# Rotary attention stage of a two-layer decoder: the clip-and-causal pass and the exponential take an earlier place in the frame

## The chip, the cores and the metric

The kernel runs on one core of a Trainium2 chip. The metric is the device time of one execution in microseconds (us), lower being better. Three timed runs of the kernel before gave 3401.52, 3405.44 and 3408.87 us; the median is 3405.44 us.

## The reference, cut to what matters

The kernel computes a decoder of two layers for 32 sequences of 112 tokens with 256 features. Each layer has a self attention, a cross attention to a context of 375 rows, and a mixture of experts. The change touches only the self attention of the second layer, which the kernel calls `RotaryAttention`. Its reference is:

```python
def _L1_attn_ref(x, W_DQ, W_UQ, W_QR, W_DKV, W_UK, W_UV, W_KR, W_O):
    # x: the layer-normalised stream, 32 x 112 x 256; 16 heads of 16 features, 8 of them rotary ones beside
    c_q = x @ W_DQ                      # 64 wide
    Qc, Qr = heads(c_q @ W_UQ), rope(heads(c_q @ W_QR))
    c_kv = x @ W_DKV                    # 64 wide
    Kc, V = heads(c_kv @ W_UK), heads(c_kv @ W_UV)
    Kr = rope((x @ W_KR)[:, None])      # one for all heads
    scores = einsum('bhqd,bhkd->bhqk', concat(Qc, Qr), concat(Kc, Kr))
    scores = clip(scores, -80.0, 80.0)
    scores = where(causal, scores, -inf)
    weights = softmax(scores / sqrt(24), axis=-1)
    attn = einsum('bhqk,bhkd->bhqd', weights, V)
    return merge(attn) @ W_O            # added to x by the caller
```

## The kernel before, in words

The stages of the decoder follow one another, with a barrier of all engines between them. `RotaryAttention` is one such stage, from about 1567 to 1877 us of the profiled span. It is streamed: sequence b passes through 17 named pieces, and a frame is one pass through the list of pieces, each for a sequence of its own. A piece of age a works in frame e on sequence b = e - a. There are 32 sequences and ages up to 4, so there are 36 frames. Four are written out in front, 28 run in a loop and four follow to drain; a piece whose sequence does not exist in a frame is left out.

The order is written out by hand in the list `Flow` (line 1464). There is no planner. Every engine walks through the same list and does its own share of each piece, so the list sets the order inside each engine's queue, and semaphores join the engines. For the change these shares matter:

- TensorE, in the order of the list: `scores` (age 2, 32 small matmuls, L1503), `q` (L1521), `turnk` (L1528, the rotary turn of the key part), `onT` (L1540), `heads` (age 3, probabilities times values, L1229), `kc` (L1521), `xT` (the transpose of the normalised input, L859), `turnq` (L1528), `v` (L1531), `c` and `kr` (L1513), `project` (L1282), `back` (L1265).
- VectorE: `stats` (L761 to L763, layer-norm statistics), `turnk` (L1595 to L1598), `scale` (L772, the normalised input that `xT` transposes), `bound` (L1583, the clip and the causal mask of all scores of a sequence in one instruction), `kc` (L1602, which adds the turned key part and frees the bank), `turnq` (L1588 to L1592), `project` (L1306), `back` (L1299, L1301).
- ScalarE: copies out of the banks, all at L885 (`q`, `onT`, `heads`, `xT`, `v`, `c`, `kr`), and `exp` (L1563, the exponential of all clipped scores of a sequence).
- GpSimd computes only the reciprocal root of the variance (L767), and SyncE has nothing to do in this stage.

Matmul results go to a ring of four banks of PSUM. The pieces `stats`, `scale`, `scores`, `bound` and `exp` take no bank of the ring. The other twelve take the banks in turn in the order of the list: `q`, `kc` and `c` the first, `turnk`, `xT` and `kr` the second, `onT`, `turnq` and `project` the third, `heads`, `v` and `back` the fourth. A piece on TensorE waits until the piece before it in its bank has been read out (`claim`, line 218). So `c` waits for VectorE's `kc`, and `v` waits for ScalarE's copy of `heads`. Where a sequence does not exist, TensorE still claims the bank and passes it on (`skip`, line 225). The scores have four banks of their own; `scores` of one sequence waits for `bound` of the sequence before it.

Of the kernel before, what the change touches and what calls it, by code (L numbers as in the profile page):

```python
# [138 lines left out]
class Chain:  # L139
# [3 lines left out]
    def __init__(self, eng, sem, once=None):  # L143
        self.eng, self.sem, self.once = eng, sem, once
        self.base = self.n = self.k = 0
# [580 lines left out]
class Phase:  # L726
# [3 lines left out]
    scale = 1.0  # L730
# [157 lines left out]
class LatentAttention(Phase):  # L888
# [4 lines left out]
    scale = XD ** -0.5 * XD ** -0.5  # L893
# [415 lines left out]
class CausalAttention(Streamed):  # L1309

    tag = "a0"
    scale = HD ** -0.5
# [142 lines left out]
class RotaryAttention(Streamed):  # L1455
# [4 lines left out]
    scale = 24 ** -0.5  # L1460

    def __init__(self, nc, G, W):
        super().__init__(nc, G, W)
        self.plan = Flow(4, [("stats", 0), ("scores", 2), ("q", 1), ("turnk", 1), ("onT", 4), ("scale", 0), ("heads", 3),
                             ("bound", 2), ("kc", 1), ("xT", 0), ("turnq", 1), ("v", 1), ("c", 0), ("kr", 0), ("exp", 2),
                             ("project", 4), ("back", 3)])

    def allocate(self, sb, sem):
# [141 lines left out]
class ContextAttention(Streamed):  # L1610

    tag = "x1"
    scale = HD ** -0.5
# [503 lines left out]
class RelativeAttention(Streamed):  # L2117
# [3 lines left out]
    scale = HD ** -0.5  # L2121
# [1014 lines left out]
```

How the kernel before makes its waits and increments, by code:

```python
    def link(self, ins):  # L168
        self.eng.wait_ge(self.sem, self.inc(ins))
# [1 line left out]
    def link_apart(self, ins):  # L171
        ins.then_inc(self.once, 1)
        self.eng.wait_ge(self.once, 1)
        self.eng.sem_clear(self.once)
# [24 lines left out]
def at_least(eng, sem, n):  # L201
    if not isinstance(n, int) or n > 0:
        eng.wait_ge(sem, n)
# [26 lines left out]
    def take(self, eng, c, e):  # L231
        eng.wait_ge(self.full[c % self.size], self.count(c, e) + 1)
        return self.banks[c % self.size]
# [4 lines left out]
    def emptied(self, eng, c, e):  # L238
        eng.wait_ge(self.free[c % self.size], self.count(c, e) + 1)
# [96 lines left out]
        @block.sync  # L336
        def _(sp):
            sp.dma_start(low["q"][0][:], t["q_aT"].rearrange("(g i) r d -> (i r) g d", i=2)).then_inc(loaded["q"], 16)
            sp.wait_ge(low_zeroed, 1)
            for i in range(2):
                sp.dma_start(low["q"][1][64 * i:64 * (i + 1), :, HD * i:HD * (i + 1)],
                             t["L0_attn_q_b"].rearrange("(g i) r d -> i r g d", i=2)[i]).then_inc(loaded["q"], 16)
            q = NB // 4
            for i in range(4):
                sp.dma_start(G["X"][0:T, i * q:(i + 1) * q, :],
                             t["x"].rearrange("b t d -> t b d")[:, i * q:(i + 1) * q, :]).then_inc(small, 16)
            sp.wait_ge(small, 64)
# [1 line left out]
        @block.scalar  # L349
        def _(act):
            act.dma_start(low["k"][0][:], t["k_aT"].rearrange("(g i) r d -> (i r) g d", i=2)).then_inc(loaded["k"], 16)
            act.wait_ge(low_zeroed, 2)
            for i in range(2):
```

## Time and profile before

| | us |
|---|---|
| median of three timed runs | 3405.44 |
| lowest and highest of them | 3401.52, 3408.87 |
| profiled execution, first to last instruction (span) | 3418.2 |
| first instruction of VectorE in the stage | 1567.07 |
| last instruction of VectorE in the stage | 1876.22 |
| one frame in the steady part | 9.0 to 9.1 |

The profiled execution is one run of its own. The profile gives its time from the first to the last instruction, 3418.2 us, and no separate time for what lies around this span. The timed runs were not profiled. A frame is the distance from the first matmul of `scores` to the first of the next frame.

### The profile page before, as it was taken

The numbers are of one execution on the slowest core, as the hardware profiler recorded it, in microseconds if no ns is written. First come the engines' busy times: TensorE is split into PE (matmuls) and PEld (weight loads), VectorE is DVE, ScalarE is ACT, GpSimd is POOL, SyncE is SP. The second block draws the span as 40 slices with busy tenths as digits, with TensorE's granted clock in tenths as the row PEclk, the third lists the DMA queues.
The fourth block names the chain that finished last, engine by engine and source line by source line (L and its number), as shares of the span: only waits on it lengthen the run. The fifth ranks groups of instructions, "written<-read, shape, count | busy, mean of one in ns | idle before, by whom it ended". The sixth has DMA issues, their size and how long they took to land. (4 is left out here: it accounts for less than half of the span.)

```text
span 3418.2 us, 78608 instructions
## 1 busy us (share of the span) xinstructions
PE 3017.6 (88%) x28488; PEld 2122.1 (62%) x28488; DVE 2357.3 (69%) x4873; ACT 1668.7 (49%) x3240; POOL 836.4 (24%) x1093
## 2 busy tenths in 40 slices
PE   6997999999999987998998799999997999955771
PEld 6886555555555555666776466666665877744661
DVE  5997566666666654676786566666663989965666
ACT  3775555555555551333444244444443877742440
POOL 0000344444444440000000100000000144445551
PEclk9998999999999997999999799999997999977996
DMA  8000555545555530000000333323322777755557
GB/s 194 0 0 2 146 145 145 144 142 144 144 145 145 145 92 1 1 0 1 0 0 2 71 68 68 70 63 68 69 55 70 218 224 227 223 169 169 156 158 233
DMA packets 316466, 351.64 MB, mean 103 GB/s; under 512 B 104552, under 2 KB 290032, under 8 KB 316112
## 3 DMA queue, kind: packets, MB, share of 16 engines
q1 hardware_dynamic: 175456, 173.66, 19.4%
q10 hardware_dynamic: 127776, 141.34, 14.9%
q0 software_dynamic: 13008, 33.56, 2.9%
q8 instruction: 151, 2.47, 0.3%
q14 instruction: 75, 0.61, 0.1%
HBM read 109.49 MB, written 207.08 MB: 93 GB/s over the span
## 5 line engine op out<-in xcount | busy, mean ns | idle before, releaser
L1090 ACT ACTIVATE x_probs<-x_held,x_minus_top 112x488 f32<-112x488 f32 x256 | 177.5, 694 | 281.8 <-DVE x_minus_top L1144 281.8
L1863 DVE TENSOR_REDUCE x_top<-x_scores 112x2 f32<-112x750 f32 x256 | 231.1, 935 | 118.7 <-PE x_scores L1720 114.3
L767 POOL TENSOR_TENSOR x_rstd<-x_var,g_minus_half 112x1 f32<-112x1 f32 x128 | 74.3, 580 | 743.6 <-DVE x_var L763 743.6
L966 POOL TENSOR_TENSOR x_probs<-x_probs,x_inverse 112x488 f32<-112x488 f32 x256 | 250.9, 1002 | 10.0
L1005 PE MATMUL x_ring<-w_xkv,x_kv 128*122 128x512 f32 x512 | 242.4, 596 | 1.2 <-PEq L229 1.2
L998 PE MATMUL x_ring<-x_kv,w_xkv 128*128 128x488 f32 x512 | 233.7, 589 | 1.8 <-ACT x_kv L1065 1.1
L1138 DVE SCALAR_TENSOR_TENSOR x_held<-x_scores,x_keep 112x976 f32<-112x976 f32 x128 | 150.4, 1175 | 108.1 <-PE x_scores L1018 100.0
L1829 ACT ACTIVATE x_probsT<-x_scores 125x1792 f32<-125x1792 f32 x96 | 159.9, 1665 | 79.4 <-PE x_scores L1739 79.4
L961 POOL TENSOR_TENSOR x_inverse<-x_sums,x_minus_one 112x2 f32<-112x2 f32 x128 | 94.8, 740 | 419.3 <-ACT x_probs L1090 419.3
L1720 PE MATMUL x_scores<-x_slots 32*112 32x375 f32 x1024 | 171.5, 538 | 27.1 <-DVE x_top L1863 14.0
L767 POOL TENSOR_TENSOR a_rstd<-a_var,g_minus_half 112x1 f32<-112x1 f32 x64 | 35.3, 551 | 586.4 <-DVE a_var L763 586.4
L2873 POOL DMA_INDIRECT expert_replies<-m_rows,m_reply_of x143 | 139.8, 978 | 111.7 <-ACT m_rows L2965 74.9
L998 PEld LDWEIGHTS x_ring<-x_kv,w_xkv 128*128 128x128 f32 x512 | 92.8, 191 | 117.4 <-issue 111.6
L885 ACT ACTIVATE x_v<-x_ring 122x512 f32<-122x512 f32 (+1 forms) x224 | 112.6, 503 | 107.7 <-PE x_ring L1005 85.6
L2751 DVE SCALAR_TENSOR_TENSOR g_residual<-m_out,m_gate,g_residual 112x256 f32 (+1 forms) x256 | 108.0, 478 | 66.2 <-PE m_out L2587 64.6
L1143 DVE TENSOR_REDUCE x_top<-x_held 112x2 f32<-112x976 f32 x128 | 149.8, 1170 | 4.4
L1005 PEld LDWEIGHTS x_ring<-w_xkv,x_kv 128*122 128x122 f32 x512 | 89.6, 185 | 93.4 <-issue 92.9
L885 ACT ACTIVATE x_probsT<-x_ring 122x448 f32<-122x448 f32 x256 | 124.9, 545 | 44.9 <-PE x_ring L1026 44.8
L1026 PEld LDWEIGHTS x_ring<-g_constants,x_probs 112*122 112x122 f32 x1024 | 109.7, 140 | 46.2 <-issue 35.4
L1018 PE MATMUL x_scores<-x_k,x_q 64*112 64x488 f32 x512 | 130.4, 607 | 1.0 <-PEq L229 1.0
L1043 PEld LDWEIGHTS x_ring<-x_probsT,x_v 122*64 122x64 f32 x2048 | 101.3, 139 | 47.3 <-issue 47.3
L1026 PE MATMUL x_ring<-g_constants,x_probs 112*122 112x112 f32 x1024 | 121.4, 262 | 6.9 <-POOL x_probs L966 4.3
(417 smaller groups left out, 7545.4 us busy)
## 6 DMA issues: line engine op xcount, KB each, us to landing
expert_slots<-d_empty ACTq DMA_DIRECT2D x32, 3612.0 KB, 14.4
by_position<-r_by_position SPq DMA_DIRECT2D x64, 784.0 KB
r_bias<-by_position SPq DMA_DIRECT2D x64, 392.0 KB
m_rows<-expert_slots SPq DMA_DIRECT2D x143, 129.0 KB
x_kq_swapped<-x_kq_raw ACTq DMA_DIRECT2D x64, 243.5 KB
x_slots<-x_kq SPq DMA_DIRECT2D x512, 30.4 KB
m_rows<-expert_replies SPq DMA_DIRECT2D x32, 448.0 KB, 8.7
w_ctx<-in_ctx SPq DMA_DIRECT2D x32, 375.0 KB
```

Of the source, the lines that this page charges most:

```text
L885: self.ring.freed(self.nc.scalar.activation(dst, src_of(bank), ACT.Copy), c)
L966: self.nc.gpsimd.tensor_tensor(probs, probs, self.inverse[0:T, u:u + 1].to_broadcast([T, XK]), ALU.mult).then_inc(self.weighted, 1)
L998: ins = nc.tensor.matmul(bank[:, 0:XK], W["xkv"][:, f, m * P:(m + 1) * P], self.kv[:, f, :], start=(f == 0), stop=(f == DC - 1))
L1005: ins = nc.tensor.matmul(bank[0:XCK, :], self.kv[:, f, i * XCK:(i + 1) * XCK], W["xkv"][:, f, 512:1024], start=(f == 0), stop=(f == DC - 1))
L1026: ins = nc.tensor.transpose(bank[0:XCK, i * T:(i + 1) * T], self.probs[u % 6][0:T, i * XCK:(i + 1) * XCK], self.const("ident", T)[:, 0:T])
L1090: nc.scalar.activation(self.probs[u % 6][0:T, :], self.held[m % 2][0:T, i, :], ACT.Exp, scale=self.scale, bias=self.minus_top[0:T, m % 2, ...
L1138: nc.vector.scalar_tensor_tensor(self.held[m % 2][0:T, :, :], self.scores[0:T, 1024 * (m % 2):1024 * (m % 2 + 1)].rearrange("t (i c) -> t ...
L1143: chain.link(nc.vector.tensor_reduce(self.top[0:T, m % 2, :], self.held[m % 2][0:T, :, :], AX_X, ALU.max))
L1720: ins = nc.tensor.matmul(self.scores[0:T, 512 * a:512 * a + S2], slots[slot, g, S2:KQ], slots[slot, g, 0:S2], start=True, stop=True)
L1829: self.nc.scalar.activation(self.probsT[0:CK, i, :, :], self.scores[0:CK, :].rearrange("t (a c) -> t a c", c=512)[:, :, 0:HG * T], ACT.Exp ...
L1863: nc.vector.tensor_reduce(self.top[0:T, g, 2 * half:2 * half + 2], self.scores[0:T, 1024 * half:1024 * (half + 1)].rearrange("t (a c) -> t ...
L2873: pool.indirect_dma_start(replies[:, :], bass.IndirectOffsetOnAxis(reply_of[:, j:j + 1], 0), rows[:, R + j % R, 0:D], None).then_inc(repli ...
```

## The change

In the list of pieces `bound` moves from behind `heads` to behind `q`, and `exp` moves from behind `kr` to in front of `heads`. The other fifteen pieces keep their order among one another, `turnq` too, and all ages stay. Since neither of the two takes a bank of the ring, every piece keeps its bank, and TensorE's order is unchanged. On VectorE the order was stats, turnk, scale, bound, kc; it becomes stats, bound, turnk, scale, kc. On ScalarE it was q, onT, heads, xT, v, c, kr, exp; it becomes q, onT, exp, heads, xT, v, c, kr. No instruction is added or removed.

```diff
@@ -1461,8 +1461,8 @@
     def __init__(self, nc, G, W):
         super().__init__(nc, G, W)
-        self.plan = Flow(4, [("stats", 0), ("scores", 2), ("q", 1), ("turnk", 1), ("onT", 4), ("scale", 0), ("heads", 3),
-                             ("bound", 2), ("kc", 1), ("xT", 0), ("turnq", 1), ("v", 1), ("c", 0), ("kr", 0), ("exp", 2),
+        self.plan = Flow(4, [("stats", 0), ("scores", 2), ("q", 1), ("bound", 2), ("turnk", 1), ("onT", 4), ("scale", 0),
+                             ("exp", 2), ("heads", 3), ("kc", 1), ("xT", 0), ("turnq", 1), ("v", 1), ("c", 0), ("kr", 0),
                              ("project", 4), ("back", 3)])
```

## Rows read from the trace of the kernel before

**Rows 1.** The page, busy time of each engine over the span.
```profile
PE 3017.6 (88%) x28488; PEld 2122.1 (62%) x28488; DVE 2357.3 (69%) x4873; ACT 1668.7 (49%) x3240; POOL 836.4 (24%) x1093
```

**Rows 2.** Windows: one in the stage, two in later stages; the columns are named.
```profile
core 0: us, PE busy (x) PEld busy (x) DVE busy (x) ACT busy (x) POOL busy (x), PEclk, DMA share, GB/s
1642.00:1678.00 36.00, 33.88 (x424) 26.88 (x423) 28.86 (x60) 16.64 (x33) 2.20 (x4) 1.00 0.00 0
2820.00:2880.00 60.00, 53.72 (x697) 43.51 (x696) 54.67 (x110) 46.23 (x69) 28.51 (x45) 0.97 0.75 216
3180.00:3240.00 60.00, 46.59 (x284) 36.34 (x282) 39.73 (x140) 24.66 (x70) 35.08 (x36) 1.00 0.53 159
```

**Rows 3.** Waits from 1606 to 1858 us: in total, times, longest.
```profile
PE a_ring L1513 <- DVE a_k L1602: 13.0, 27, 0.5
```

**Rows 4.** Timeline of TensorE, one frame: start, duration, line, operation [idle before].
```profile
1715.17 1.05 PE L1503 MATMUL a_scores<-a_q,a_k 32*112 32x112 f32 x32
...
1719.54 0.36 PE L859 MATMUL a_ring<-g_constants,a_xn 112*128 112x112 f32 x2
...
1720.50 0.59 PE L1531 MATMUL a_ring<-w_av,a_c 128*112 128x256 f32 x2
1721.52 0.70 PE L1513 MATMUL a_ring<-a_xT,w_ac 128*128 128x112 f32 x4 [0.43 <-DVE a_k L1602]
...
1722.71 1.12 PE L1282 MATMUL a_ring<-w_ao,a_normedT 128*112 128x256 f32 x4
...
1724.20 1.05 PE L1503 MATMUL a_scores<-a_q,a_k 32*112 32x112 f32 x32
```

**Rows 5.** Timeline of TensorE: scores of the frames e = 4 and e = 32.
```profile
1597.15 1.05 PE L1503 MATMUL a_scores<-a_q,a_k 32*112 32x112 f32 x32
...
1851.24 1.05 PE L1503 MATMUL a_scores<-a_q,a_k 32*112 32x112 f32 x32
```

**Rows 6.** Timeline of TensorE, v and c in frame 3, with no wait between.
```profile
1594.28 0.59 PE L1531 MATMUL a_ring<-w_av,a_c 128*112 128x256 f32 x2
1595.01 0.70 PE L1513 MATMUL a_ring<-a_xT,w_ac 128*128 128x112 f32 x4
```

**Rows 7.** Timeline of VectorE in the frame of rows 4.
```profile
1716.70 0.15 DVE L763 TENSOR_SCALAR a_var<-a_mv 112x1 f32<-112x1 f32 x1
1717.56 0.28 DVE L1595 TENSOR_TENSOR a_kr_plain<-a_kr,g_constants 128x112 f32<-128x112 f32 x1 [0.71 <-PE a_ring L1528]
...
1718.59 0.41 DVE L772 TENSOR_SCALAR a_xn<-g_residual,a_mv,a_rstd 112x256 f32 x1
1718.92 2.02 DVE L1583 SCALAR_TENSOR_TENSOR a_clipped<-a_scores,g_constants 112x1792 f32<-112x1792 f32 x1
1720.85 0.61 DVE L1602 TENSOR_TENSOR a_k<-a_ring,a_kr_turned 128x448 f32<-128x448 f32 x1
```

**Rows 8.** Timelines of VectorE and TensorE, first frame: scale, and xT behind it.
```profile
1568.67 0.41 DVE L772 TENSOR_SCALAR a_xn<-g_residual,a_mv,a_rstd 112x256 f32<-112x256 f32 x1 [0.67 <-POOL a_rstd L767]
...
1569.23 0.38 PE L859 MATMUL a_ring<-g_constants,a_xn 112*128 112x112 f32 x2 [4.68 <-DVE a_xn L772]
```

**Rows 9.** Timeline of ScalarE in the frame of rows 4: heads and exp.
```profile
1718.83 0.54 ACT L885 ACTIVATE a_heads_raw<-a_ring 128x448 f32<-128x448 f32 x1 [0.66 <-PE a_ring L1229]
...
1722.92 1.69 ACT L1563 ACTIVATE a_probsT<-a_clipped 112x1792 f32<-112x1792 f32 x1
```

**Rows 10.** Timelines of ScalarE and TensorE, frame e = 33, the last with scores.
```profile
1862.28 0.54 ACT L885 ACTIVATE a_heads_raw<-a_ring 128x448 f32<-128x448 f32 x1 [0.57 <-PE a_ring L1229]
1863.03 1.70 ACT L1563 ACTIVATE a_probsT<-a_clipped 112x1792 f32<-112x1792 f32 x1 [0.20 <-DVE a_clipped L1583]
...
1863.97 1.09 PE L1282 MATMUL a_ring<-w_ao,a_normedT 128*112 128x256 f32 x4 [1.82 <-PEq L229]
```

**Rows 11.** Timeline of TensorE: q at the stage's start and in the steady frame.
```profile
1571.97 1.91 PE L1521 MATMUL a_ring<-a_c,w_aq 128*128 128x112 f32 x8
...
1716.16 1.15 PE L1521 MATMUL a_ring<-a_c,w_aq 128*128 128x112 f32 x8
```

## The prediction

> **What bounds the kernel now.** I read the page first: TensorE is busy for 88% of the span, VectorE for 69% [rows 1]. That is an average over stages, so I went to the windows of this one: in 36 us TensorE is busy for 33.88, VectorE for 28.86, ScalarE for 16.64, and the granted clock is 1.00 [rows 2]. The reader is to see that a frame here is as long as TensorE's work plus what TensorE waits for. The waits say what that is: in the steady part `c` waits for `kc`, the read-out on VectorE that frees its bank, 13.0 us in 27 frames, 0.48 each [rows 3]. No other wait of TensorE of any length is listed there.
>
> Then I read one frame on each engine. Let S be the start of `scores`. TensorE starts `xT` at S+4.37, `v` at S+5.33, `c` at S+6.35 after a wait of 0.43, `project` at S+7.54, and the next `scores` at S+9.03 [rows 4]. Without a wait `c` starts 0.73 after `v` [rows 6]; here it is 1.02. So the wait costs about 0.3 of a frame. From e = 4 to e = 32 there are 28 frames in 254.09 us, 9.075 each [rows 5]. Without any wait the path from `xT` to the next `scores` is 0.96 + 0.73 + 1.19 + 1.49 = 4.37 us, and the frame would be 8.74.
>
> **Part 1: the clip in front of `turnk` and `scale`.** On VectorE the clip takes 2.02 us, and its successor starts 1.93 after it [rows 7]. At present it stands behind `scale`, and all that it delays is `kc`, hence the wait above. The change puts it in front of the three instructions of `turnk` and of `scale`, and what hangs on these is `xT` on TensorE.
>
> - Where can the clip start? VectorE reaches it when the statistics are done. The last of them starts at S+1.53 and takes 0.15 [rows 7]; with about 0.05 to the next start that is S+1.73. Other frames of the same trace have it up to 0.07 later, so I take S+1.77. The scores are there by then, since their matmuls end at S+1.05 [rows 4]; the clip waits for nothing.
> - `turnk` starts 1.93 later, at S+3.70. From the first of `turnk` to `scale` is 1.03, and `scale` takes 0.41 [rows 7]: it ends at S+5.14. Before, it ended at S+3.83.
> - TensorE's `xT` needs that result. In the first frame, the only place where it waited for it, it started 0.15 after the end of `scale` [rows 8]. I take S+5.28, between 5.20 (no delay, and `turnk` at the short end) and 5.40 (the longer `turnk` and the late statistics).
> - TensorE is in order. Its `xT` stood at S+4.37, so it now waits for 0.91 us, and `turnq`, `v`, `c`, `kr`, `project`, `back` and the next `scores` are queued behind it. The wait of `c` for `kc` goes in return: `kc` starts about 0.4 behind `scale` and takes 0.61 [rows 7], so it ends near S+5.7, and `c` comes at S+6.97.
> - The new frame: 5.28 + 4.37 = 9.65 us, against 9.075: +0.575 us. The next frame starts from the same relation, because the statistics follow `back`, which moves with TensorE. So the loss repeats and is not caught up.
>
> The frames with a clip, a `scale` and a full set of neighbours are e = 4 to 31, 28 of them: 28 x 0.575 = +16.1 us; with the ends 5.20 and 5.40 it is 28 x 0.495 = +13.9 and 28 x 0.695 = +19.5. In e = 2 and 3 some pieces are missing, VectorE reaches the clip when the scores end, and the gain on `kc` and the loss on `xT` are each below 1 us and of opposite sign; the same in e = 32, where no `scale` exists. I take 0 for the three together, between -1.5 and +1.5.
>
> **Part 2: the exponential in front of the copy of `heads`.** The exponential takes 1.69 us and ScalarE is busy less than half of the stage [rows 2, 9]. It now waits for a clip that ends at S+3.79, so it ends at S+5.5, and the copy of `heads` (0.54), which used to start at S+3.66 [rows 9], ends at S+6.1. Queued behind it are the copies of `xT`, `v`, `c` and `kr`. TensorE's `v` needs the bank of `heads`: it would come at S+5.28 + 0.96 = S+6.24 anyway, so the late copy is hidden, with 0.1 us to spare. The cover is the wait for `xT`; if that were gone, `v` would stand at about S+6.15 instead of 5.33, and the frame would be 6.15 + 0.73 + 1.19 + 1.49 = 9.56, which is +0.48. The copy of `xT` is half the size of that of `heads` and ends by S+6.6, ahead of `c` at S+6.97. The earlier exponential brings nothing in return: TensorE's `heads` of the next frame did not wait for it [rows 3].
>
> In the draining part the cover is missing. In e = 33 no `xT` exists; the copy of `heads` started at 1862.28, the exponential at 1863.03, as soon as the clip was done, and `project` stood at 1863.97, having passed the bank of `heads` on its way [rows 10]. With the exponential first, the copy starts when it ends, at about 1864.65, 2.37 later, and `project` and the rest of the drain are later by as much. The bounds are 0 (if the drain has a slack that I do not see) and 2.5. I take +2.35, once.
>
> **The sum.** 16.1 + 0 + 2.35 = +18.5 us. The profiled span of 3418.2 us would become 3436.7; the profiled execution stands 12.8 us above the median of the timed runs, of which no part belongs to the change. On the median: 3405.44 + 18.5 = **3424 us**, +0.54%. With the ends of the terms: from 13.9 - 1.5 + 0 = +12.4 to 19.5 + 1.5 + 2.5 = +23.5, that is 3418 to 3429.
>
> **Rivals.**
> - *The clip goes out of the way of `kc` and nothing takes its place* (faster). In its favour: this is the only wait of TensorE that the steady part has [rows 3]. The frame would be 8.74, which is -0.34, and 28 of them give -9.5; with the drain, 3405.4 - 9.5 + 2.35 = 3398 us. It decides at `xT`: `scale` must end by S+4.25. That needs a clip started by S+0.9, before the scores of the frame are complete at S+1.05, and a copy of `heads` done by S+5.3. I see no way for both; 6%.
> - *VectorE reaches the clip as soon as the scores are complete* (no change). If the statistics were done by S+1.1, `xT` would come at S+1.1 + 1.93 + 1.03 + 0.41 + 0.14 = S+4.61, and the frame would be 8.98, -0.1: -2.7 + 2.35 leaves 3405 us. Against it: the statistics follow `back`, which is the piece just before `scores` on TensorE. 6%.
> - *Only ScalarE's order costs*: `scale` reaches TensorE sooner than I think, and `v` waits for the bank of `heads`. 28 x 0.48 = +13.4, with the drain +15.8: 3421 us; with a copy 0.15 sooner +11.6: 3417. 8%.
> - *TensorE's clock.* The waits take TensorE's busy share from 94% to some 89%. A later stage at 89.5% has a granted clock of 0.97, another at 78% has 1.00 [rows 2]. At 0.97, 6% of the stage's 270 us (16 us) would be at 1.2 GHz; the eight matmuls of `q` took 1.91 us there and 1.15 in the steady frame, at 2.4 [rows 11], so at most 16 x 0.4 = 6.5 us come on top: 3431 us. 5%. The Trainium skill, "TensorE: Matmul & The Clock Gate", section "A second HAM failure mode: psum-queue depth-cycling", says that a kernel which cycles through PSUM banks, with short idle gaps of TensorE between the groups, made the gate go to and fro between its levels. By that rule the new gap in every frame would be a danger of its own; the present gap in every frame did not lower the clock, so this trace does not bear it out.
> - The Trainium skill, "Perfetto Trace Analysis", section "Optimization Strategies", says that when the matmul engine idles behind another engine, it is the blocking engine's work that is to be improved. Read on the one wait that the stage shows, this is the first rival, 3398 us; my sum disagrees, since the instruction taken from `kc` lands in front of `xT`.
>
> **How the numbers follow.** The forecast has 75%; the rivals have 6, 6, 8 and 5. What differs by 0.2% (6.8 us) from 3405.4 can be told from no change by this measurement. The forecast, the third rival and the clock are slower by more than that: 88%, of which I take 1 off for ends that come together, 87%. No change: 6% and that one, 7%. Faster: 6%. The range is 3411 to 3432: it holds the forecast's own 3418 to 3429, the third rival, most of the clock's case, and 2 or 3 us for the scatter of the median.
>
> **What would show it.** In the changed kernel's profile: a frame of 9.5 to 9.75 us; in TensorE's waits some 0.9 us a frame of `xT` (L859) for VectorE's `scale` (L772), and nothing of `c` for `kc`; `turnk` (L1595) no longer waiting on TensorE; the copy of `heads` ending near S+6.1; the drain longer by over 2 us. A wait of `v` (L1531) for L885 instead of the one at L859 would mean the third rival. The prediction is wrong if `xT` starts before S+4.6, or if the other stages move by more than 3 us.

## The result, and the profile after

Over 18 runs each, the changed kernel has a median of 3415.27 us and the kernel before one of 3408.87 us. The ratio is 1.0021, 95% interval 1.0013 to 1.0029: slower by 7.2 us (4.4 to 9.9). The 7.2 us are this ratio applied to the median before; the two medians differ by 6.4. The forecast was +18.5 us. The direction was right and the size was 2.6 times too large. The median of 3415.27 us lies in the stated range of 3411 to 3432 and below the 3418 to 3429 that the forecast's own terms gave.

The timelines say where it lies. I cut the stage at the first instruction of VectorE, the first `scores` (e = 2), those of e = 4, 32 and 33, and the last instruction of VectorE (us, from the timelines of the two profiled executions):

| part of the stage | before | after | difference | forecast |
|---|---|---|---|---|
| start, frames 0 and 1 | 13.45 | 13.68 | +0.23 | 0 |
| frames 2 and 3 | 16.63 | 15.86 | -0.77 | 0 |
| frames 4 to 31, 28 of them | 254.09 | 257.73 | +3.64 | +16.1 |
| frame 32 | 8.61 | 8.16 | -0.45 | 0 |
| drain, from the last `scores` (e = 33) | 16.37 | 21.05 | +4.68 | +2.35 |
| sum | 309.15 | 316.48 | +7.33 | +18.5 |

The sum lies in the interval of the timed runs, so nothing outside the stage is needed to explain them. That it agrees to 0.1 us is luck: some 2.3 us of it are a part of the drain that differs between executions of the same kernel, as e8 below shows. The changed execution's whole span, 3406.1 us, is shorter than the 3418.2 of before, and a second profiled execution of the same changed kernel (e8) has 3418.7. Single executions scatter by more than the change is worth, and this is the reason for reading the stage and not the span.

The waits of the changed kernel from 1606 to 1858 us, all of TensorE's (us in total, times, longest):

```profile
PE a_ring L859 <- DVE a_xn L772: 17.2, 27, 0.8
PE a_ring L1282 <- DVE a_q_turned L1589: 0.6, 1, 0.6
```

The wait of `c` for `kc` [rows 3] is gone and `xT` waits for `scale`, as forecast. Next, one frame on TensorE, to be held against [rows 4] (start, duration, line, operation, idle before):

```profile
1702.60 1.05 PE L1503 MATMUL a_scores<-a_q,a_k 32*112 32x112 f32 x32
...
1707.91 0.41 PE L859 MATMUL a_ring<-g_constants,a_xn 112*128 112x112 f32 x2 [0.79 <-DVE a_xn L772]
...
1708.93 0.59 PE L1531 MATMUL a_ring<-w_av,a_c 128*112 128x256 f32 x2
1709.36 0.59 PE L1513 MATMUL a_ring<-a_xT,w_ac 128*128 128x112 f32 x4
...
1710.47 1.12 PE L1282 MATMUL a_ring<-w_ao,a_normedT 128*112 128x256 f32 x4
...
1711.96 1.05 PE L1503 MATMUL a_scores<-a_q,a_k 32*112 32x112 f32 x32
```

`xT` starts at S+5.31 (S is the start of `scores`); I had said 5.28. But `c` follows `v` after 0.43 us, where [rows 6] had 0.73, `project` follows `c` after 1.11, where I had 1.19, and the next `scores` follow `xT` after 4.05 us, where I had 4.37. This is the reading that failed. In the other frame of the loop's body `xT` comes at S+5.02, with a wait of 0.50. The difference between the two kinds of frame is on VectorE, here the end of the statistics and the clip in both:

```profile
1695.06 0.15 DVE L763 TENSOR_SCALAR a_var<-a_mv 112x1 f32<-112x1 f32 x1
1695.14 2.02 DVE L1583 SCALAR_TENSOR_TENSOR a_clipped<-a_scores,g_constants 112x1792 f32<-112x1792 f32 x1
...
1704.21 0.15 DVE L763 TENSOR_SCALAR a_var<-a_mv 112x1 f32<-112x1 f32 x1
1704.40 2.03 DVE L1583 SCALAR_TENSOR_TENSOR a_clipped<-a_scores,g_constants 112x1792 f32<-112x1792 f32 x1
...
1707.45 0.41 DVE L772 TENSOR_SCALAR a_xn<-g_residual,a_mv,a_rstd 112x256 f32 x1 [0.22 <-DVE a_kr_turned L1598]
```

The clip starts at S+1.60 and S+1.80 in turn. In the short kind it starts 0.08 us after the last of the statistics started, in the long kind 0.19; I had allowed 0.2 in all frames. Two other gaps between VectorE's instructions, ahead of the statistics and ahead of `scale`, add about 0.1 us each in the long kind. `scale` ends at S+4.97 and S+5.26, 5.115 on average, against 5.14 said, and `xT` starts 0.05 us behind it in both kinds; I had taken 0.14 from the first frame [rows 8].

The drain on ScalarE and TensorE, to be held against [rows 10]; the last `scores` start at 1858.06:

```profile
1861.23 1.70 ACT L1563 ACTIVATE a_probsT<-a_clipped 112x1792 f32<-112x1792 f32 x1 [1.21 <-DVE a_clipped L1583]
1862.84 0.53 ACT L885 ACTIVATE a_heads_raw<-a_ring 128x448 f32<-128x448 f32 x1
```

```profile
1864.51 1.51 PE L1282 MATMUL a_ring<-w_ao,a_normedT 128*112 128x256 f32 x4 [4.04 <-PEq L229]
```

`project` comes 6.45 us after the `scores`, before it was 4.12: +2.33, the forecast's 2.35. The drain grew by 4.68. The rest, 2.35 us, lies behind that `project`: from there to the last instruction of VectorE are 14.60 us, and before it was 12.25. It goes with TensorE's clock. The four matmuls of the next `project` took 2.02 us in the changed kernel (first) and 1.09 in the kernel before (second):

```profile
1871.75 2.02 PE L1282 MATMUL a_ring<-w_ao,a_normedT 128*112 128x256 f32 x4 [1.72 <-PEq L229]
```

```profile
1869.40 1.09 PE L1282 MATMUL a_ring<-w_ao,a_normedT 128*112 128x256 f32 x4 [1.72 <-PEq L229]
```

In windows of 10 us (TensorE's busy time is the first figure behind the window, the granted clock the third from the end) the changed kernel fell to the lower level inside the drain,

```profile
1860.00:1870.00 10.00, 5.06 (x62) 3.41 (x54) 2.31 (x4) 2.51 (x4) 0.00 (x0) 0.75 0.00 0
```

and the kernel before only near its end:

```profile
1860.00:1870.00 10.00, 5.56 (x111) 4.25 (x112) 3.77 (x6) 3.50 (x5) 0.00 (x0) 1.00 0.01 2
```

### The profile page after: what moved, and what is told of

It reads as the page before. It is cut to its first block and busy times, and to the rows that moved or that the text cites. A ratio compares the mean times of both kernels' runs of the same rounds, so it can differ in the third digit from the quotient of the medians.

```text
span 3406.1 us, 78623 instructions
## 1 busy us (share of the span) xinstructions
PE 3009.7 (88%) x28488; PEld 2118.7 (62%) x28488; DVE 2358.8 (69%) x4873; ACT 1663.3 (49%) x3240; POOL 835.4 (25%) x1093
```

## The experiments

Frames are means over e = 4 to 31, stages and drains are cut as in the table above. Ratios are to the kernel before on the same chip. The two kernels with half a clip (e3, e6) leave out the clip and the mask of half of the scores, so they compute something else; they measure what a shorter clip would give.

| kernel | ratio (95%) | frame | drain | stage |
|---|---|---|---|---|
| before | 1 | 9.075 | 16.37 | 309.15 |
| changed | 1.0021 (1.0013 to 1.0029) | 9.205 | 21.05 | 316.48 |
| e1, only the clip moved | 1.0033 (1.0021 to 1.0045) | 9.199 | 17.78 | 314.30 |
| e2, only the exponential moved | 1.0229 (1.0214 to 1.0244) | 11.415 | 22.40 | 386.61 |
| e3, before with half a clip | 0.9948 (0.9934 to 0.9961) | 8.346 | 17.79 | 288.39 |
| e4, clip behind turnq | 1.0072 (1.0060 to 1.0084) | 9.560 | 19.31 | 331.38 |
| e5, clip cut in two | 0.9950 (0.9934 to 0.9966) | 8.457 | 19.48 | 293.87 |
| e6, changed with half a clip | 0.9947 (0.9930 to 0.9963) | 8.376 | 21.67 | 292.86 |
| e7, exponential behind heads | 1.0013 (1.0001 to 1.0024) | 9.198 | 19.53 | 314.56 |
| e8, changed once more | 1.0027 (1.0016 to 1.0037) | 9.196 | 22.44 | 317.43 |

**e1: only the clip moves.**

```diff
-("stats", 0), ("scores", 2), ("q", 1), ("turnk", 1), ("onT", 4), ("scale", 0), ("heads", 3), ("bound", 2), ...
+("stats", 0), ("scores", 2), ("q", 1), ("bound", 2), ("turnk", 1), ("onT", 4), ("scale", 0), ("heads", 3), ...
```

> Only the clip moves (bound behind q); the exponential stays at the end of the frame. Theory A, now held: the late transpose of the input (xT waits for scale, which stands behind the clip) sets the frame, 9.2 us on average as in the changed kernel, and the drain of 21.05 us in the changed kernel falls back to the 16.4 us of before, since it was lengthened by the exponential standing in front of the copy of heads. Stage 312 to 313 us against 309.15 before and 316.48 in the changed kernel; time +3 us (+0.1%) on before. Theory B: the changed kernel's frame was shorter than predicted because the exponential's earlier place gives something back; then the frame is 9.5 or more here and the time +12 us.

The frame is 9.199 us: the clip alone sets it. The stage is 5.15 us longer than before, against 3 to 4 expected. The drain, 17.78 us and not 16.4, has 1.4 of the miss; its four matmuls of the second `project` took 1.79 us, so the lower clock came earlier here too. The other part is frame 3, which takes 9.50 us instead of 8.40. There the clip waits for the first exponential, which on its old place comes late and behind a table load:

```profile
1584.99 1.28 ACT L1563 ACT_TABLE_LOAD   x1
1586.28 1.70 ACT L1563 ACTIVATE a_probsT<-a_clipped 112x1792 f32<-112x1792 f32 x1
```

```profile
1588.08 2.02 DVE L1583 SCALAR_TENSOR_TENSOR a_clipped<-a_scores,g_constants 112x1792 f32<-112x1792 f32 x1 [1.95 <-ACT a_probsT L1563]
```

So the exponential's earlier place has one use, once: with it frame 3 takes 8.00 us. The timed ratio (7 to 15 us) lies above what the stage shows (5 us); I have no cause for the rest.

**e2: only the exponential moves.**

```diff
-("scale", 0), ("heads", 3), ("bound", 2), ("kc", 1), ... ("kr", 0), ("exp", 2), ...
+("scale", 0), ("exp", 2), ("heads", 3), ("bound", 2), ("kc", 1), ... ("kr", 0), ...
```

> Only the exponential moves (in front of heads); the clip keeps its old place. Theory A: ScalarE is in order, the exponential waits for a clip that ends at S+5.8, the copy of heads ends near S+7.9, and v waits for the bank of heads until S+8.0; the frame is 8.0 + 0.43 + 1.11 + 1.48 = 11.05 us and the time +55 us. Theory B (ScalarE has slack for it, since it is busy less than half of the stage): the frame stays within 0.3 us of 9.08.

A stage of +77 us, where 55 were expected; the mechanism is the expected one. TensorE, `v` in one frame:

```profile
1713.82 0.69 PE L1531 MATMUL a_ring<-w_av,a_c 128*112 128x256 f32 x2 [2.48 <-ACT a_heads_raw L885]
```

Many frames took 10.77 us (11.05 expected), but about every third took 12 to 12.6 and the one of e = 4 took 14.05. In those the lower clock shows (the four matmuls of `project` took 1.91 us at 1658.27 and 1.03 at 1670.32), and the granted clock of the stage is 0.96, no longer 1.00:

```profile
1640.00:1680.00 40.00, 29.83 (x365) 23.59 (x364) 27.24 (x54) 15.37 (x29) 1.65 (x3) 0.96 0.00 0
```

**e3: the order of before, half a clip.** The decisive one. The clip and the mask of the second half of the scores are left out, and the exponential reads the first half twice, so that its size stays:

```diff
-    nc.vector.scalar_tensor_tensor(self.clipped[0:T, :, :], ...[:, :, 0:HG * T], -80.0, bc(const("keep1T", T), 1, HS), ...
+    nc.vector.scalar_tensor_tensor(self.clipped[0:T, 0:2, :], ...[:, 0:2, 0:HG * T], -80.0, bc(const("keep1T", T), 1, 2), ...
```

> The kernel before, in its own order, with the clip done on two of the four banks of scores only (2.02 us becomes about 1.0); the exponential reads these twice and keeps its size. So kc frees its bank about 1 us sooner and c need not wait. Theory A: from v to c without a wait is 0.43 us, the kernel before loses 0.64 us a frame to that wait, and the frame becomes 8.43; 28 x 0.64 = 18 us less. Theory B, the reading of the prediction: from v to c without a wait is 0.73 us, the wait costs 0.34 us, the frame becomes 8.74 and the time 9.5 us less.

8.346 us a frame, even below the 8.43 of theory A and far from 8.74. From 1606 to 1828 us no wait of TensorE is listed at all, and this is its uninterrupted run from `xT` on:

```profile
1707.99 0.36 PE L859 MATMUL a_ring<-g_constants,a_xn 112*128 112x112 f32 x2
...
1708.95 0.59 PE L1531 MATMUL a_ring<-w_av,a_c 128*112 128x256 f32 x2
1709.39 0.59 PE L1513 MATMUL a_ring<-a_xT,w_ac 128*128 128x112 f32 x4
...
1711.98 1.05 PE L1503 MATMUL a_scores<-a_q,a_k 32*112 32x112 f32 x32
```

From `xT` to the next `scores` are 3.99 us. The kernel before thus lost 0.73 us a frame to the clip in front of `kc`, not 0.34. 28 x 0.73 = 20.4, and the stage is 20.8 us shorter (13 to 23 by the timed runs). Half a clip also takes 0.94 us off VectorE's whole work of a frame, so e3 alone doesn't part the wait from the amount of work; e5 does.

**e4: the clip moves the other way, behind `turnq`.**

```diff
-("heads", 3), ("bound", 2), ("kc", 1), ("xT", 0), ("turnq", 1), ("v", 1), ...
+("heads", 3), ("kc", 1), ("xT", 0), ("turnq", 1), ("bound", 2), ("v", 1), ...
```

> The kernel before with the clip moved the other way, behind turnq; all else in its place. Neither kc nor scale stands behind the clip now. The clip runs from about S+7.4 to S+9.4, the exponential until S+2.7 of the next frame, where TensorE's heads waits for it about 0.25 us. Theory A: frame 8.43 + 0.27 = 8.7, time -10 us (-0.3%). Theory B, with 8.74 as the frame without waits: 9.0, -2 us. A third outcome: VectorE's project and back, now queued behind the clip, hold the statistics, scale and xT, and the frame is not shorter than 9.08.

Slower, in turn 9.45 and 9.55 us a frame; the mean of 9.56 holds one of 11.13 at e = 4, where the granted clock was still at 0.85. The time fits the third outcome and the mechanism fits none of the three: the wait is another one, that the expectation forgot. There is one set of scores, so TensorE's `scores` of the next frame wait for the clip:

```profile
PE a_scores L1503 <- DVE a_clipped L1583: 28.2, 26, 1.1
```

The clip has to lie between the end of one frame's `scores` and the start of the next. At the early end it costs `xT`, in the middle `kc`, at the late end the next `scores`.

**e5: the clip in two instructions, one of them in VectorE's idle time.** The order is otherwise that of the kernel before, the exponential included. The last two lines of the cut are in `scores`, which now counts two clips for a sequence; the exponential does the same:

```diff
+("q", 1), ("boundA", 2), ("turnk", 1), ("onT", 4), ("scale", 0), ("heads", 3), ("boundB", 2), ("kc", 1), ...
+        elif name in ("boundA", "boundB"):
+            half = slice(0, 2) if name == "boundA" else slice(2, 4)
...
-            at_least(pe, self.clipped_ready, b)
+            at_least(pe, self.clipped_ready, 2 * b)
```

> The order of before, with the clip cut into two instructions of two banks of scores each, 1.08 us apiece by the run with half a clip: the first behind the statistics, in the 0.71 us in which VectorE waited for turnk's matmul, the second where the clip stood. Theory A (the frame is the uninterrupted 8.35 us plus what kc, or scale, comes late): first half S+1.7 to 2.8, scale ends S+4.15, xT needs it at 4.37; second half ends S+5.15, kc S+5.7, and c comes at S+5.76 to 5.8. Frame 8.35 to 8.45, 28 x 0.65 = 18 us less than before, time -0.5%. Theory B (VectorE's total work, 7.4 us and its gaps, sets the frame): 9.0 or more, no gain. A middle outcome: project waits for the turned queries, frame 8.6 to 8.8, -8 to -13 us.

Theory A to the edge of its range: 8.457 us, in turn 8.35 and 8.57. It is 0.5% faster than the kernel before and with it faster than the changed one. VectorE does more work here than before (1.09 us twice for 2.02) in a shorter frame. In the short kind of frame `scale` ends at 1707.66 and `xT` starts at 1708.00: not late. Here is the long kind, VectorE first and then TensorE (the line numbers stand up to three higher than before):

```profile
1716.21 1.09 DVE L1586 SCALAR_TENSOR_TENSOR a_clipped<-a_scores,g_constants 112x896 f32<-112x896 f32 x1
1717.21 0.62 DVE L1605 TENSOR_TENSOR a_k<-a_ring,a_kr_turned 128x448 f32<-128x448 f32 x1
```

```profile
1716.35 0.41 PE L859 MATMUL a_ring<-g_constants,a_xn 112*128 112x112 f32 x2
...
1717.37 0.59 PE L1532 MATMUL a_ring<-w_av,a_c 128*112 128x256 f32 x2
1717.88 0.70 PE L1514 MATMUL a_ring<-a_xT,w_ac 128*128 128x112 f32 x4
1718.42 0.61 PE L1514 MATMUL a_ring<-a_xT,w_akr 128*128 128x112 f32 x4
```

`scale` ends at 1716.30, and `xT` starts at S+4.37, no later than in the short kind, with 0.06 us more to `v`. But `kc` ends at 1717.83, and `c` starts at 1717.88, 0.51 us behind `v` and not 0.43; `kr` follows `c` after 0.54 us and not 0.43. Most of the 0.22 us is again a wait for the bank of `kc`, and again none is listed. So VectorE's total never set the frame; what it had in front of `xT` or of `kc` did.

**e6: the changed kernel with half a clip** (the edit of e3 on the changed order).

> The changed kernel with the clip done on two of the four banks of scores only (1.08 us instead of 2.02), the exponential reading these twice at its full size. Theory A: scale ends near S+4.1, before xT would start, so the changed order costs nothing in a frame and the frame is 8.35 as in the kernel before with half a clip; what is left of the changed order's cost is the drain and start. Against that run (0.9948 of before) it is 2 to 4 us more: 0.995 to 0.997. Theory B: the changed order costs also through ScalarE, v waiting for the copy of heads; then the frame is 8.6 or more and the time within 0.3% of before.

The frame is 8.376 us. With 0.94 us less in front of `scale`, the changed order costs 0.03 us in a frame, ScalarE's order included. Its stage is 4.5 us longer than that of e3, 3.9 of it in the drain; the timed runs do not part the two.

**e7: the changed kernel with the exponential behind the copy of `heads`.**

```diff
-("exp", 2), ("heads", 3), ("kc", 1), ...
+("heads", 3), ("exp", 2), ("kc", 1), ...
```

> The changed kernel with the exponential behind the copy of heads instead of in front of it; the clip stays early. Theory A: frame 9.2 as in the changed kernel, since ScalarE's order has no part in it; the copy of heads in the last frame with scores no longer waits for the exponential, so the drain is 17 to 18 us instead of 21.05. Stage 312 to 314 us against 309.15 before and 316.48 changed, time +0.1 to +0.15% on before. Theory B: the longer drain of the changed kernel is the lower clock of that execution and not the order; then the drain is 21 here too.

The frame is 9.198 as expected. The drain is 19.53 us, between the two answers, and the stage 314.56. Its `project` stands at S+4.13, as before the change, so the 2.33 us of the order are gone:

```profile
1860.78 1.05 PE L1503 MATMUL a_scores<-a_q,a_k 32*112 32x112 f32 x32
...
1864.91 1.81 PE L1282 MATMUL a_ring<-w_ao,a_normedT 128*112 128x256 f32 x4 [1.72 <-PEq L229]
```

But the lower clock began in this drain at this very `project` (1.81 us for its four matmuls, 1.09 in [rows 10]), behind an idle time that was no longer than before (1.72 us against 1.82).

**e8: the changed kernel once more.**

> The changed kernel once more beside the others, for a comparison on the same chip. Theory A: stage +7 us on before, frame 9.2, drain near 21; time +0.2%. If the 21 us of the drain came from a chance fall of the clock, it will differ here.

Frame and stage repeat to 0.01 and 1 us, the drain is 22.44 this time, with `project` again 6.45 us after the `scores`. So of the drain's growth the order's part (2.3 us) is fixed; the clock's part differs from execution to execution. In the six kernels whose copy of `heads` stands ahead of the exponential the drains went from 16.4 to 19.5 us, in the four with the exponential in front from 21.1 to 22.4. The kernel before is the shortest of the six, so its drain flattered it by 1 to 3 us in the table of the result.

## Why the prediction was right or wrong

- **What bounds the kernel:** right in kind (TensorE's run plus one wait for `kc`), wrong in size, and this is the step that failed. I took the 0.73 us from `v` to `c` in frame 3 [rows 6] for a distance without a wait, because no wait was listed there. The trace of the kernel before has the reason in a row that I did not put beside it:

```profile
1594.34 0.61 DVE L1602 TENSOR_TENSOR a_k<-a_ring,a_kr_turned 128x448 f32<-128x448 f32 x1
```

  It ends at 1594.95, and `c` starts at 1595.01: the bank had just been freed. `c` waited there too. From `v` to an unhindered `c` are 0.43 or 0.44 us (the changed kernel, e3), less than the 0.59 shown as the duration of `v`. So a matmul's shown end lies behind the moment at which the next one may start, and the 0.59 us covered more than half of the wait of 0.30. The price of 0.34 us for the wait was too small by this 0.30 and by 0.08 more, since `project` follows a `c` that waited after 1.19 us and one that did not after 1.11. "The path from `xT` is 4.37 us, and the frame would be 8.74" should have been 3.99 to 4.05, and 8.35. The listed 13.0 us [rows 3] stood for some 20.
- **Part 1, where the clip can start and when `xT` comes:** right in mechanism, a little off in size. S+5.28 was said; it is S+5.31 and S+5.02 in turn, 5.165 on average. That is 0.115 us a frame, 3.2 us in all, and 0.09 of it is the step from the end of `scale` to `xT`, 0.05 us where I had taken 0.14. The path behind `xT` is 0.33 us shorter than said, 9.2 us in all. Together these are the 12.5 us between +16.1 and +3.64.
- **What goes in return:** the removal of the wait at `kc` was worth 0.73 us a frame and I had it at 0.34. The new frame, 9.205, is 8.35 and 0.86 of late `xT`; the two costs nearly cancel (e3, e6).
- **Part 2, the exponential is hidden in a frame:** right (e1 and e7 have the frame of the changed kernel to 0.01). Its cover is the wait for `xT`, and no run takes that away from a whole clip that starts early, so the 9.56 us for a lost cover were not tested. e2 is another case and costs more: there the clip still stands behind `scale`, `v` starts at S+7.98, and the frame is 10.77 us.
- **The drain:** the 2.35 us were right (2.33 measured, and gone in e7). Not foreseen: the lower clock came earlier in this drain, another 2.35 us. That the longer idle time of TensorE brought it (4.04 us ahead of `project`, 1.82 before) is not shown: in e7 the idle time was as before, and the clock fell at this `project` all the same. Each drain is read from one execution.
- **Frames 2, 3 and 32:** -1.2 us, inside the bound of 1.5.
- **The rivals:** none came true. The first needs `xT` on time; with a shorter clip e6 shows it, and its frame is 8.376 us, not the 8.74 at which the rival was priced. For the third no wait of `v` is listed, and `v` follows `turnq` after 0.77 us as in e3 (0.76). The clock stood at 1.00 from 1606 to 1858 us. "A frame of 9.5 to 9.75 us" as the sign of the forecast was not met; the sign at `xT`, and nothing at `c`, was. By the prediction's own sign of being wrong, other stages moving by more than 3 us, the two profiled executions can't judge: outside this stage they differ by 19 us, and the two of the changed kernel by 12.

## What to carry to other kernels

Measure an uninterrupted distance on TensorE from start to start, and only after checking that the bank or operand it needs was not freed just then; "no wait listed" does not mean that there was none, and a listed wait is too short by what the shown end of the matmul before it covers. Here a second sign was the matmul behind: it followed a `c` that had waited after 0.53 or 0.54 us and an unhindered one after 0.43. When a long instruction moves within an in-order queue, write down both what it used to delay and what it will delay, each against TensorE's start without any wait: here they were 0.73 and 0.86 us, and the gain was in neither place but in cutting the instruction, so that the first half fits in idle time of its queue and the second holds `kc` up hardly at all. A drain has none of the covers of the steady frame; sum it by itself.

## What the runs showed of the hardware

- In the changed kernel TensorE had a listed wait of 0.5 to 0.8 us in every frame of 9.2, and the granted clock was 1.00 from 1606 to 1858 us. In e2 it waited for 2.5 us in every frame of 10.8, and the granted clock was 0.92 to 0.96 in windows of 40 us from 1640 us on, part of the time thus at the lower level of 1.2 GHz; frames of 10.77 us became 12 to 12.6 about every third time. An estimate from the frames gives it 18 of the 77 us of e2: 28 x (11.415 - 10.77). The Trainium skill, "TensorE: Matmul & The Clock Gate", section "A second HAM failure mode: psum-queue depth-cycling", describes such a to and fro between the two levels, in a kernel that cycles through PSUM banks with short idle gaps. By that rule, the trace of e2 agrees, and that of the changed kernel does not show it.
- Loop bodies are not equal: the two frames unrolled in one pass of the loop differ by 0.11 us before and 0.29 us after the change, each time in the small gaps between VectorE's instructions (after the change 0.08 or 0.19 us from the statistics to the clip; before, 0.41 or 0.52 us from the last instruction of `turnk` to `scale`, start to start). Why the gaps differ is open.
- The clip on half the columns takes 1.09 us, the whole 2.02, so some 0.16 us of the duration is fixed. From its start to that of the next instruction are 1.00 us for the half and 1.93 for the whole: in VectorE's queue cutting the clip costs 0.07 us.
